# Attention block on one core: M jobs, comparisons, Newton steps and the turns of q in another order

## The reference

```
xn = layernorm(x)
q, k = elu(xn @ Wq) + 1, elu(xn @ Wk) + 1          # 1024 columns
v = xn @ Wv
z = q . sum_n(k) + 1e-6                            # per head
kv = k^T @ v                                       # 64 x 64 per head
x = x + ((q @ kv) / z) @ Wo + bo
y = square(relu(layernorm(x) @ W_fc^T)) @ W_proj^T
# five steps: mem = 0.9 * mem + y - (mem > 1); count += mem > 1
x = x + count / 5
```

## Time and profile before

| | |
|---|---|
| timed runs, median of 3 | 1065.61 us (1065.39 to 1065.88) |
| profiled execution | 1062.29 us, its span 1060.5 us |
| TensorE | 1031.4 us busy, 97% of the span |
| VectorE | 930.8 us, 88% |
| ScalarE | 704.3 us, 66% |
| GpSimd | 634.6 us, 60% |
| DMA queue of SP | 42.3% of 16 engines' span |

### The profile page before, as it was taken

How to read it: one execution, slowest core, us unless ns; L and a number is a source line. 1 busy time by engine, 2 the same in 40 slices (tenths; PEclk the granted TensorE clock), 3 DMA queues, 4 the chain that set the end, 5 groups by cost and what they waited for, 6 DMA issues and landing times.

```text
span 1060.5 us, 20207 instructions
## 1 busy us (share of the span) xinstructions
PE 1031.4 (97%) x7364; PEld 691.3 (65%) x7364; DVE 930.8 (88%) x1775; ACT 704.3 (66%) x1145; POOL 634.6 (60%) x404
## 2 busy tenths in 40 slices
PE   8999999999999999899999999999999999999997
PEld 4444444444444466678786777877777787878786
DVE  7889888898889698899989899999989999998956
ACT  6788677777767648457575666666666565757553
POOL 1443434364445477576777657777776777677733
PEclk9999999999999999999999999999999999999999
DMA  5546443224324433335444444445434443544341
GB/s 140 134 128 148 108 119 95 65 66 115 99 60 91 113 77 83 77 85 121 103 112 92 101 91 109 88 100 120 100 86 105 111 100 85 120 102 85 70 81 45
DMA packets 263091, 104.24 MB, mean 98 GB/s; under 512 B 217296, under 2 KB 260432, under 8 KB 262992
## 3 DMA queue, kind: packets, MB, share of 16 engines
q1 hardware_dynamic: 262992, 102.96, 42.3%
HBM read 33.69 MB, written 16.79 MB: 48 GB/s over the span
## 4 chain that ended last, share of the span: by engine, by line
PE 75%; DVE 15%; ACT 3%; issue 2%; DMA 2%; SPq 1%; POOL 1%; ACTq 0%; DVEq 0%; POOLq 0%
PE proj L553 25%; PE acc L709 13%; PE acc L581 12%; PE acc L683 12%; PE acc L667 11%; DVE feat L1066 2%; DVE feat L992 2%; DVE spikes L1146 2%; DVE zsum L1070 2%; DVE xnat L987 2%; ACT feat L763 1%; DVE xn L982 1%; DVE newt L1191 1%; DMA xT<-xnat 1%; PE acc L639 1%
## 5 line engine op out<-in xcount | busy, mean ns | idle before, releaser
L759 ACT ACTIVATE feat<-proj 128x1024 f32<-128x1024 f32 x124 | 126.7, 1022 | 219.2 <-PE proj L553 219.2
L1265 POOL TENSOR_TENSOR qT<-qT,feat 128x1024 f32<-128x1024 f32 x60 | 141.5, 2358 | 181.0 <-DVE xnat L987 157.4
L1300 POOL TENSOR_TENSOR h<-h_f,h 128x512 f16<-128x512 f32 x128 | 151.1, 1201 | 110.4 <-ACT h L885 110.4
L709 PE MATMUL acc<-wpT,h 128*128 128x256 f16 x1536 | 179.3, 274 | 6.9 <-DVE spikes L1146 6.8
L683 PE MATMUL acc<-xn2T,wfcT 128*128 128x256 f16 x1536 | 178.0, 273 | 2.8 <-DMA xn2T<-xnat 1.7
L553 PE MATMUL proj<-wk,xT 128*128 128x512 f16 x768 | 176.1, 379 | 3.7 <-DMA xT<-xnat 3.6
L581 PE MATMUL acc<-feat,xnat 128*128 128x512 f16 x768 | 176.2, 379 | 0.0
L667 PE MATMUL acc<-m_all,qT 128*128 128x256 f16 x1488 | 172.6, 273 | 3.0 <-DVE x L1161 1.8
L683 PEld LDWEIGHTS acc<-xn2T,wfcT 128*128 128x128 f16 x1536 | 150.1, 98 | 32.4 <-issue 2.1
L553 PE MATMUL proj<-wq,xT 128*128 128x512 f16 x720 | 165.2, 379 | 2.6 <-DVE feat L992 2.1
L709 PEld LDWEIGHTS acc<-wpT,h 128*128 128x128 f16 x1536 | 150.1, 98 | 27.0 <-DVE spikes L1146 7.9
(11 more groups left out here) (81 smaller groups left out, 1159.0 us busy)
## 6 DMA issues: line engine op xcount, KB each, us to landing
x_t<-in_L_attn_x_dram SPq DMA_DIRECT2D x128, 128.0 KB, 2.3
xT_spill<-xT SPq DMA_DIRECT2D x64, 128.0 KB, 2.0
out_dram<-out_t SPq DMA_DIRECT2D x64, 128.0 KB, 2.1
xT<-xT_spill SPq DMA_DIRECT2D x60, 128.0 KB, 2.4
ks_all<-ks_rows SPq DMA_DIRECT2D x4, 512.0 KB, 4.8
m_all<-in_L_attn_Wk_dram SPq DMA_DIRECT2D x4, 256.0 KB, 4.3
xT<-xnat SPq DMA_TRANSPOSE x64, 2.4
m_all<-in_L_ffn_W_fc_dram SPq DMA_DIRECT2D x4, 256.0 KB, 3.5
```

The lines of the kernel that those rows point to most:

```text
L709: mm = pe.matmul(y_at(n), h[:, pair % 2, left, f, u * P:(u + 1) * P], wpT[:, right, f::FB, :], start=(i == 1), stop=(i == FB * len(PRODUCTS)))
L1265: pool.tensor_tensor(kacc[:, b % 2, :], kacc[:, b % 2, :], k_feat(n), ALU.add).then_inc(k_added, 1)
L1300: pool.tensor_tensor(lo, h_f[:, k % 4, :], hi, ALU.subtract).then_inc(h_lo, 1)
```

## The change

There are seven edits.

1. Border tiles (n = 33 and 49): k's exp stands ahead of xn's high part on ScalarE, and k's elu directly behind `normalise_a` on VectorE.
2. q is turned in two DMA transposes, high half and low half, each with its own wait; the semaphore counts 32 for a tile in place of 16. For the early q tiles the high half is issued one iteration earlier.
3. SP loads xT of tile 4 ahead of the first x loads of the second part, and tile 5 in between.
4. In the passage by hand `o_tile(4)` stands ahead of the first `f1_half`, and on ScalarE `q_hi_tile(6)` ahead of `h_hi_of(0)` and `q_hi_tile(7)` behind `relu_of(2)`.
5. In step 10 the five comparisons of tile 0 and its write stand ahead of the low parts of xn2.
6. `newton_pair` uses operations on one column, alternating between the two tiles, in place of operations on two columns.
7. The two last M jobs move by one tile and stand at the end of a step on TensorE, behind f2; VectorE makes the elu of the next q tile before the end of that step, and the low parts of M behind the multiplication by the k sum.

```diff
+        def border(n):
+
+            return n in GUESTS and n % BT == 1
...
-        LATE = {7: ("kv", B - 1, 0), 25: ("m", B - 1, 0), 28: ("m", B - 1, 1)}
+        LATE = {7: ("kv", B - 1, 0), 26: ("m", B - 1, 0), 29: ("m", B - 1, 1)}
...
-            def turn_q(n):
-                sp.wait_ge(q_lo, n + 1)
+            def turn_q(n, part):
+                sp.wait_ge(q_lo if part else q_hi, n + 1)
...
-                sp.dma_start_transpose(qT_at(n), q_both(n)).then_inc(qT_ready[n % 4], 16)
+                sp.dma_start_transpose(qT_at(n)[:, part * PAIRS:(part + 1) * PAIRS, :], q_half(n, part)
+                                       ).then_inc(qT_ready[n % 4], 16)
+
+            def turn_q_both(n):
+                turn_q(n, HI)
+                turn_q(n, LO)
...
-                if q_guest(n, 13) is not None:
-                    turn_q(q_guest(n, 13))
+                for part in (HI, LO):
+                    if q_guest(n, 12 + part) is not None:
+                        turn_q(q_guest(n, 12 + part), part)
...
+            load_first_xT(4)
+            sp.wait_ge(ln1.norm, TILES)
+            load_x_b(0)
+            load_x_b(1)
+            load_first_xT(5)
+            load_x_b(2)
+            load_x_b(3)
+            load_first_xT(6)
+            load_first_xT(7)
...
-                pe.wait_ge(qT_ready[n % 4], 16 * (n // 4 + 1))
+                pe.wait_ge(qT_ready[n % 4], 32 * (n // 4 + 1))
...
             q_tile(7)
+            o_tile(4)
             for i in range(4):
                 pe.wait_ge(w_turned[i], 64)
             f1_half(0)
             q_tile(8)
             f1_half(1)
-            o_tile(4)
             q_tile(9)
...
             for t in STEPS:
-                if t + 1 in LATE:
-                    guest_job(*LATE[t + 1])
                 if live(t + 1):
                     q_tile(t + 1)
...
+                if t + 2 in LATE:
+                    guest_job(*LATE[t + 2])
...
                 if n:
                     k_hi_tile(n - 1)
+                if border(n):
+                    k_exp_tile(n)
                 if live(n + 2):
                     xn_hi_a(n + 2)
...
+            q_hi_tile(6)
             h_hi_of(0)
-            q_hi_tile(6)
             q_exp_tile(8)
             relu_of(1)
             h_hi_of(1)
-            q_hi_tile(7)
             q_exp_tile(9)
             relu_of(2)
+            q_hi_tile(7)
             h_hi_of(2)
...
                 if live(n + 2):
                     normalise_a(n + 2)
+                if border(n):
+                    k_elu_tile(n)
                 if n:
                     k_lo_tile(n - 1)
...
+                for stage in range(3):
+                    for i in range(2):
+                        u = (2 * pair + i) % 4
+                        r0, p, q, r1 = seed[:, u:u + 1], newt[:, u, 0:1], newt[:, u, 1:2], newt[:, u, 2:3]
+                        if stage == 0:
+                            done = dve.tensor_scalar(p, mv[:, u, 1:2], LN_EPS, r0, ALU.add, ALU.mult)
+                        else:
+                            dve.wait_ge(ln2.newton, 6 * pair + 2 * stage - 1 + i)
+                            if stage == 1:
+                                done = dve.tensor_scalar(q, p, r0, -0.5, ALU.mult, ALU.mult)
+                            else:
+                                done = dve.tensor_scalar(r1, q, 1.5, r0, ALU.add, ALU.mult)
+                        done.then_inc(ln2.newton, 1)
...
                 spiking = at(f2_step, t - 1)
+                if t == FILLED + 1:
+                    for k in range(5):
+                        spike_step(0, k)
+                    write_out(0)
                 for n in at(o_step, t - 2):
                     if n % 2:
                         lo_pair(n // 2)
                 for k in range(5):
-                    if live(t):
+                    if live(t) and not (k == 0 and t + 1 in LATE):
                         Q_STEPS[k](t)
-                    if k == 0 and t + 1 in LATE:
+                    if k == 1 and t + 1 in LATE:
                         m_lo_job(*LATE[t + 1][1:])
...
+                if t + 2 in LATE:
+                    q_elu_tile(t + 1)
                 for n in at(o_step, t - 1):
                     if n % 2:
                         normal_pair(n // 2)
```

More of the change, by code:

```diff
@@ L235, in q_half @@
             return q16_early[n % 2][:, part, :] if n < EARLY else feat16[:, n % 2, part, :]
-        def q_both(n):
-            halves = q16_early[n % 2] if n < EARLY else feat16[:, n % 2, :, :]
-            return halves.rearrange("p h n -> p (h n)")
         def qT_at(n):
@@ L494, in store_out, with load_first_xT @@
                 sp.dma_start(out_rows[rows(n), :], out_t[:, n % 4, :]).then_inc(out_stored[n % 4], 16)
-            sp.wait_ge(ln1.norm, TILES)
-            for n in range(4):
-                load_x_b(n)
-            for n in range(EARLY, EARLY + 4):
+            def load_first_xT(n):
                 sp.wait_ge(xnT_spilled[n % 4], 16 * CHUNKS)
@@ L506, in _ @@
             load_xT(10)
-            turn_q(4)
+            turn_q_both(4)
             load_x_b(4)
             load_x_b(5)
-            turn_q(5)
+            turn_q_both(5)
             load_x_b(6)
@@ L519, in _ @@
             load_xT(12)
-            turn_q(6)
+            turn_q_both(6)
             load_x_b(8)
-            turn_q(7)
+            turn_q_both(7)
             for t in STEPS:
@@ L534, in _ @@
                 if t > FILLED and live(t - 2):
-                    turn_q(t - 2)
+                    turn_q_both(t - 2)
                 if t == 20:
@@ L833, in q_hi_tile @@
                 if live(n - 2):
-                    act.wait_ge(qT_ready[(n - 2) % 4], 16 * ((n - 2) // 4 + 1))
+                    act.wait_ge(qT_ready[(n - 2) % 4], 32 * ((n - 2) // 4 + 1))
                 act.activation(q_half(n, HI), q_feat(n), ACT.Copy).then_inc(q_hi, 1)
@@ L839, in _ @@
                     k_hi_tile(n - 1)
+                if border(n):
+                    k_exp_tile(n)
                 if live(n + 2):
                     xn_hi_a(n + 2)
-                if live(n) and n - 1 not in GUESTS:
+                if live(n) and n - 1 not in GUESTS and not border(n):
                     k_exp_tile(n)
@@ L980, in normalise @@
                 u = n % 4
-                dve.wait_ge(ln.newton, 3 * (n if ln is ln1 else n // 2) + 3)
+                dve.wait_ge(ln.newton, 3 * n + 3 if ln is ln1 else 6 * (n // 2) + 5 + n % 2)
                 dve.tensor_scalar(xn[:, n % 2, :], src, mv[:, u, 0:1], newt[:, u, 2:3],
@@ L1157, in residual @@
                     for u in range(EARLY):
-                        dve.wait_ge(qT_ready[u], 16)
+                        dve.wait_ge(qT_ready[u], 32)
                 dve.wait_ge(o_done, n + 1)
@@ L1179, in newton_pair @@
             def newton_pair(pair):
-                u = 2 * pair % 4
-                r0, var = seed[:, u:u + 2], mv[:, u:u + 2, 1]
-                p, q, r1 = newt[:, u:u + 2, 0], newt[:, u:u + 2, 1], newt[:, u:u + 2, 2]
                 dve.wait_ge(ln2.seed, pair + 1)
-                dve.scalar_tensor_tensor(out=p, in0=var, scalar=LN_EPS, in1=r0, op0=ALU.add, op1=ALU.mult
-                                         ).then_inc(ln2.newton, 1)
-                dve.wait_ge(ln2.newton, 3 * pair + 1)
-                dve.scalar_tensor_tensor(out=q, in0=p, scalar=-0.5, in1=r0, op0=ALU.mult, op1=ALU.mult
-                                         ).then_inc(ln2.newton, 1)
-                dve.wait_ge(ln2.newton, 3 * pair + 2)
-                dve.scalar_tensor_tensor(out=r1, in0=q, scalar=1.5, in1=r0, op0=ALU.add, op1=ALU.mult
-                                         ).then_inc(ln2.newton, 1)
+                for stage in range(3):
[11 more added lines that the diff above has]
+                        done.then_inc(ln2.newton, 1)
             def normal_pair(pair):
@@ L1232, in _ @@
                 for k in range(5):
-                    if live(t):
+                    if live(t) and not (k == 0 and t + 1 in LATE):
                         Q_STEPS[k](t)
-                    if k == 0 and t + 1 in LATE:
+                    if k == 1 and t + 1 in LATE:
                         m_lo_job(*LATE[t + 1][1:])
+                    if t > FILLED + 1:
+                        for n in spiking:
+                            spike_step(n, k)
+                if t > FILLED + 1:
                     for n in spiking:
-                        spike_step(n, k)
-                for n in spiking:
-                    write_out(n)
+                        write_out(n)
+                if t + 2 in LATE:
+                    q_elu_tile(t + 1)
                 for n in at(o_step, t - 1):
```

## The result

| | before | changed |
|---|---|---|
| timed runs, median | 1065.50 us (4 runs, 1063.69 to 1065.88) | 1048.95 us (4 runs, 1048.78 to 1049.66) |
| profiled execution | 1062.29 us | 1048.78 us, span 1047.0 |

The ratio is 0.9849, 95% interval 0.9832 to 0.9866: 16.5 us by the medians, 13.5 between the two profiled executions. The forecast was 1052.3 as a median and 1049.0 in its own terms. The 3.32 us between the profiled and the timed runs of before, which the prediction carried over, did not come with it: the two agree within 0.2 in the changed kernel.

What follows compares the result with a forecast made beforehand. TensorE, busy 97% of the span, was the bound: only its holes and restart costs could be won, with VectorE close behind. Terms summed to -13.3: 1049.0 in its own terms, 1052.3 as median; range 1048.0 to 1059.

Steps and rivals of the forecast that it cites:

- Term 1: Border tiles 33 and 49: the guest query projection no longer waits for the elu; -1.9, bounds -1.9 and -0.9.
- Term 2: q turned in halves: the late turn of xn behind q tile 2 shortens; -1.1, bounds 0 and 1.43.
- Term 3: First load of xT ahead of the x_t loads: TensorE's wait for xT goes; -0.65, bounds 0 and -0.65.
- Terms 4 and 5: Filling: reordering closes two f1 waits, -3.1; comparisons of tile 0 ahead of xn's low part close f2's 4.37 wait, -3.0.
- give-back inside term 5: After f2 of tile 1 starts earlier, VectorE makes the next f2s wait: 1.8, then about 1.0; 3.0 of 6.0 with restarts.
- Term 6: One-column Newton escapes blocking by GpSimd near the end, part returning in the normalise; -1.6, bounds 0 and -3.0.
- Term 7: Late M jobs: first job's hole goes, -2.25; second's 1.50 becomes 1.9; net -2.0, bounds -3.9 and +1.
- A: VectorE becomes the bound; the first f2 hole returns nearly whole and M jobs collide; about 1058, chance 0.16.
- B: More is won: blocks near the end and at 622 dissolve as GpSimd and VectorE meet differently; 1048.0, chance 0.12.
- C: Slower: the second normalise of every pair of steps is blocked by GpSimd; +27, 1080, chance 0.05.
- D: Front part and filling: holes of terms 1 to 4 move to the next consumer; 1060.6, chance 0.05.

Runs made afterwards that it cites:

- q 8 first: Changed kernel with the two half turns of q tile 8 issued on SP ahead of the turns of xn2 for tiles 4 and 5: 1048.82 us, ratio 0.9844.
- Newton alone: Kernel before with only the one-column Newton and the count that `normalise` waits for: 1055.72 us against 1064.03, ratio 0.9924.

## Why the prediction was right, and where it was not

**The bound.** Right: TensorE's holes, with the slow group behind one, were all there was to win (18.1 us of printed waits behind the fifth k projection before, 5.0 after), and closing them made VectorE's next wait visible.

**Term 1** (-1.9) was right and stands alone: 1.9 at its two places, 2.3 when undone (0.4 of it a wait for xT at 347, which is not at its places).

**Term 2** (-1.1) was slightly mis-sized: the half turn holds SP for 1.23 and the whole hole goes (1.4). No run shows a cost in the steps, which the prediction put at 0; undoing the edit cost 0.7, less than the place is worth, because of a wait near the end that whole turns had in two kernels of three.

**Term 3** (-0.65) measured 0.7 at its place; it was not undone.

**Terms 4 and 5** failed in their attribution. The step was "of the 6.8 ... 0.9 is left for here" and "the earlier Newtons that were blocked lie in terms 4 and 5": I named the second benefit of edit 6 and gave it no number. Edit 4 was priced at 3.1, and undoing it costs 0.6; edit 5 at 3.0, and undoing it costs 0.4, which is not told from nothing. Newton alone takes the 4.37 hole to 1.39 and the group of 4.25 back to 2.79.

**The give-back inside term 5** was right in kind and near in size: 1.8 and 1.0 forecast, 1.88 and 1.42 with q 8 first. In the changed kernel itself it took another shape, 1.98 and a slow group for SP's queue, which I had not seen because I asked only what is late next on VectorE and costed SP at 0. In size the give-back was 4.0 by 452, where 3.0 was taken.

**Term 6** (-1.6) is the largest miss: right near the end (1.7), but 4.7 when undone and 7.4 alone. The rule behind it held: the 64 operations of each new kind have means of 202 to 208 ns, and the wide normalise is blocked in their place, 34.6 us in all against 26.9:

```profile
L996 DVE TENSOR_SCALAR xn<-x,mv,newt 128x256 f32<-128x256 f32 x64 | 34.6, 583 | 0.0
...
L1207 DVE TENSOR_SCALAR newt<-newt,seed 128x1 f32<-128x1 f32 x64 | 10.6, 207 | 0.0
```

The rule of the Trainium skill weighed there (SBUF — State Buffer, Who interferes with whom) says that tensor_scalar can enter a two-port mode when its operands meet certain conditions. The prediction left the conditions out and weighed it as if it held for any width, by which this edit would have been worth nothing. The runs decide for the rows: no operation on one column lasted over 0.22 us in the changed kernel, while the wide normalise was blocked, as the page has it.

**Term 7** (-2.0) was mis-sized in its second half: the first job as forecast (2.25). The second kept a wait of 0.65, not 1.9: the normalise was blocked (2.34 for the pair at 609.98), and so were the low parts at 613.24 (3.38), but of all this only 0.65 reached f2. With the restart that is 0.8, where 1.9 was taken, and 2.25 + 1.65 - 0.8 is the 3.1 that undoing it cost.

**Why the sum came out.** The terms were read off the holes of one trace, and their sum is bounded by the holes and what stands behind them, whoever closes them. The seven single terms are not seven effects: undone one at a time, six edits cost 2.3, 0.7, 0.6, 0.4, 4.7 and 3.1, in sum 11.8. With the 0.7 of term 3 that is 12.5 of the 13.7 between the two kernels' matmul times. That the sum of -13.3 met the profiled 13.5 was partly luck, since errors of 2.5 to 3.1 had opposite signs. The forecast as a median, 1052.3, missed 1048.95 by 3.4, nearly all of it the 3.32 between profile and median that was carried over and did not come.

**Rivals.** A (VectorE becomes the bound) describes the stretch from 422 to 452 but at no such price. B's number, 1048.0, was nearest among the rivals; its reason, dissolved blocks, fits only the second M job. C did not happen: no waits for comparisons in every pair of steps. D, by which the holes of terms 1 to 4 only move on, describes edit 4 in part, and edit 5, which it had counted as won.

## What to carry to other kernels

A hole's size belongs to the place, not to the edit that closes it: where two edits touch one region, price them together and test each alone, above all the one that removes a block. In the two cases tried here, moving an operation off VectorE handed its block to VectorE's next wide operation; giving an operation a form that is not blocked was what paid. When work is moved behind something, ask of every in-order queue that waits for it, the one that issues DMAs included, what stands behind that wait.

## What the runs showed of the hardware that was not expected

The granted clock fell to 0.5 after some holes and not after others of the same length. Columns of the windows view: stretch, its length, then busy us of PE, PEld, DVE, ACT, POOL, then granted clock, DMA share and GB/s. The changed kernel:

```profile
434.80:438.20 3.40, 1.42 (x14) 1.03 (x13) 3.40 (x3) 3.40 (x7) 3.40 (x2) 1.00 0.97 161
438.30:441.60 3.30, 3.30 (x18) 2.37 (x16) 3.27 (x12) 1.43 (x2) 3.30 (x4) 0.50 0.68 128
```

It is the 1.2 GHz level for 3.4 us, behind a wait of 1.98 and after 1.1 us of matmuls at 2.4 GHz, and it made the group 1.53 longer. With edit 7 undone the same group waited longer and paid nothing more:

```profile
438.20 2.79 PE L679 MATMUL acc<-m_all,qT 128*128 128x256 f16 x24 [2.26 <-DMA qT<-feat]
```

The same happened at the start of the program, where no edit acts: behind a wait of 1.98 the third k projection took 4.45 in one run (q 8 first), behind 1.85 it took 2.76 in the changed kernel:

```profile
16.55 4.45 PE L567 MATMUL proj<-wk,xT 128*128 128x512 f16 x12 [1.98 <-DMA xT<-xnat]
```

```profile
16.67 2.76 PE L565 MATMUL proj<-wk,xT 128*128 128x512 f16 x12 [1.85 <-DMA xT<-xnat]
```

Some 0.8 us of that remain at the fifth k projection. So 1.5 us behind a hole may come or stay away, and a term should carry it in its bounds, not in its middle as term 5 did. And it costs only where TensorE would not have had to wait afterwards: in the changed kernel, as told above, it cost nothing. Why the timed runs of before spread from 1063.69 to 1065.88 was not settled.

A half turn of q holds SP for 1.24 us (median of 120 issues) and lands 3.2 us after its issue (median), where the whole turn took 4.4: halving the data took off 1.2, not 2.2.

Newton's new form has another operation and another width than the old one, and which of the two frees it was not separated. Width seems to play a part, though the operands differ in more than width: the same kind of operation on 16 columns was blocked in the kernel before, where its shortest takes under 0.2:

```profile
413.50 1.19 DVE L1075 TENSOR_SCALAR zeps<-zsum 128x16 f32<-128x16 f32 x1
```
